# Mixture-of-experts phase of a fused long-convolution kernel: expert results kept in SBUF over the dispatched rows, in four chunks of groups

## The chip, the cores and the metric

One core of a Trainium2 chip runs the whole program. The metric is the device time in microseconds (us); the kernel before takes 2235.25 us, the median of three runs (2234.15 to 2236.55).

## What is computed

Two layers on x of 8192 tokens by 512, each with a residual and a layer norm. The first is a gated long convolution (a transform of length 16384, written as matrix products). The second, to which the change belongs, is a mixture of 32 x 4 = 128 small experts, in float32:

```
grouped = x.reshape(1, 256, 32, 512)                       # 256 groups of 32 tokens
logits  = einsum('bgtd,des->bgtes', grouped, controller) + tie
perm    = (logits == max(logits over t))                   # each expert takes one token of a group
dispatched   = einsum('bgtd,bgtes->bgesd', grouped, perm)  # its row, for each group and expert
inner        = relu(einsum('bgesd,desf->bgesf', dispatched, f1) + bias)   # 32 hidden values
intermediate = einsum('bgesf,esfd->bgesd', inner, f2)
out          = einsum('bgesd,bgtes->bgtd', intermediate, perm)
x = layernorm(x + out)
```

## The kernel before

The program runs four phases one behind the other, `front_phase`, `frequency_phase`, `output_phase` and `experts_phase`; each is one block in which the five engines have streams of their own, ordered by hand through semaphores. A phase begins when all streams of the last have ended.

At the end of `output_phase` the choices stand in `k_shared` (K, 128 experts by 8192 tokens): `choose(u)` on VectorE writes ones and zeros over the logits. `turn_take(v)` on TensorE transposes them to tokens by experts, `keep_took` copies these from PSUM, and `store_unit` on SyncE (SP) writes them to the scratch tensor TOOK in HBM.

`experts_phase` before works in `STEPS` = 4 steps: two halves of the groups (`GH` = 128) times two halves of the experts (`EH` = 64). A step is

- a **dispatch stage**: for each pair of token tiles `dispatch(c, j)` multiplies the tile by the choices, in two row strips of 64 (two groups in one product, so `pick` is padded with zeros by GpSimd at L1435). The result is x at the chosen tokens, turned: dimension on partitions. `keep_tile` (L1527) copies it from PSUM to `taken`.
- a **layer stage** over `QH` = 16 quads of experts: `layer1(c, i)` (L1472) 16 products in four column strips of 32, each with 128 groups as columns; `hidden` (L1580) adds the bias and cuts at zero; `layer2(c, i)` (L1484) four products of 512 columns in four row strips; `keep_out` (L1534) copies 2 x 1024 columns to `out`; SP stores 1 MB to the scratch tensor I (L1408) and loads the weights of a later quad (L1341).

From the third step on, the tiles of the first half are combined in between: `combine(m)` (L1498) multiplies rows of I, loaded back from HBM, by the choices (TAKE, stored to HBM and loaded back as well), and `add`, `moments`, `root`, `scale`, `finish` make the layer norm and ScalarE issues the store of the output. The second half is combined behind the last step. PSUM has three bank pairs `pd` for dispatch, shared with the layers, and two banks `pc` for combine.

Of the kernel before, what the change touches and what calls it, by code (L numbers as in the profile page):

```python
# [878 lines left out]
def output_phase(nc, sem, A, S, K, O):  # L879
# [5 lines left out]
    NZ, NR, NK = 3, 6, 4  # L885
    with ExitStack() as ctx:
# [3 lines left out]
        def ps(name, shape):  # L890
# [18 lines left out]
        took = [sb(f"took{s}", [P, 2, 8, ES // 2]) for s in range(NK)]  # L909
# [4 lines left out]
        pt = [ps(f"pt{s}", [P, 4, ES]) for s in range(2)] + pc  # L914
# [25 lines left out]
        def _(sp):  # L940
# [31 lines left out]
            def store_unit(u):  # L972
                for b in range(2):
                    sp.wait_ge(took_ok[b], ONE + u + 1)
                sp.dma_start(S["TOOK"][:, :, 8 * u:8 * u + 8, :].rearrange("h p m e -> p h (m e)"),
                             took[u % NK][:].rearrange("p h m e -> p h (m e)")).then_inc(took_st[u % NK], 16)

# [10 lines left out]
            for u in range(UNITS):  # L988
                store_unit(u)
            for s in range(NR):  # L990
                sp.wait_ge(x1_st[s], ONE + 16 * len(range(s, TILES, NR)))
            for s in range(NK):
                sp.wait_ge(took_st[s], ONE + 16 * UNITS // NK)
# [15 lines left out]
        def _(pe):  # L1009
# [35 lines left out]
            def turn_take(v):  # L1045
                pe.wait_ge(take_ok, ONE + UNITS + v // 2 + 1)
                if v == 2:
                    pe.wait_ge(c_used, ONE + TILES)
                if v >= 4:
                    pe.wait_ge(took_ok[v % 2], ONE + v // 2 - 1)  # L1050
                for b in range(4):
                    g = v * UG // 2 + 2 * b
                    m = pe.transpose(pt[v % 4][:, b, :], logit[:, g:g + 2].rearrange("p g r t -> p (g r t)"), ident[:])
                m.then_inc(t_ps, 1)

# [9 lines left out]
            for v in range(2 * UNITS):  # L1065
                turn_take(v)

        def keep_took(eng, copy, v):

            u, b = v // 2, v % 2  # L1070
            eng.wait_ge(t_ps, ONE + v + 1)
            if u >= NK:
                eng.wait_ge(took_st[u % NK], ONE + u // NK * 16)
            copy(took[u % NK][:, :, 4 * b:4 * b + 4].rearrange("p h m e -> p m h e"),
                 pt[v % 4][:].rearrange("p m (h e) -> p m h e", h=2)).then_inc(took_ok[b], 1)

        @block.scalar
        def _(act):
# [44 lines left out]
            for u in range(UNITS):  # L1123
                keep_took(act, nc.scalar.copy, 2 * u)

        @block.vector
        def _(dve):
# [50 lines left out]
            def choose(u):  # L1178
                half, g = u // UNITS, u % UNITS * UG
                by_group = logit[:, g:g + UG, half, :]  # L1180
                dve.wait_ge(top_ok, ONE + (half + 1) * HALF)
                dve.tensor_tensor(by_group, by_group,
                                  top[half][:, g:g + UG].rearrange("p (g a) -> p g a", a=1).to_broadcast([P, UG, GT]),
                                  ALU.is_equal).then_inc(take_ok, 1)

            for n in STEPS:
# [11 lines left out]
                for u in chosen(n):  # L1198
                    choose(u)
                    if u > UNITS:  # L1200
                        keep_took(dve, dve.tensor_copy, 2 * (u - UNITS - 1) + 1)
            keep_took(dve, dve.tensor_copy, 2 * UNITS - 1)

def experts_phase(nc, sem, A, S, K):

    GH = P
    NH = G // GH
    EH = ES // 2  # L1210
    TH = GH * GT // P
    QH = EH // 4
    NF = 4
    STEPS = NH * 2
    NO, NI, NR = 3, 2, 4
    PH = TH // 2
    ND = 3
    NX = 8
    WEIGHTS_OVER = (6, 7)
    TILES_OVER = (0, 1, 2, 3, 4, 5)  # L1220
    NP, NK = 2, 3
    NW = TH // 4
    IN_DISPATCH = (3, 6, 9, 12, 15)
    IN_LAYERS = tuple(i for i in range(QH) if i % 3 != 2)
    NT0 = NT // NH
    NL = 8
    LW = 5 * D + P
    with ExitStack() as ctx:
        def sb(name, shape, dt=F32):
            return ctx.enter_context(nc.sbuf_tensor("e_" + name, shape, dt))  # L1230

        taken = sb("taken", [P, DT * EH * GH])
        bias = sb("bias", [P, Q])
        eps = sb("eps", [P, 1])
        inter = [K[:, s * 4 * D:(s + 1) * 4 * D].rearrange("p (g d) -> p g d", g=4) for s in range(NI)]
        xt = [sb(f"xt{s}", [P, 2, D]) for s in range(2)]
        pick = [sb(f"pick{s}", [P, 2, 2 * EH]) for s in range(NP)]
        picked = [sb(f"picked{s}", [P, 4, EH]) for s in range(NK)]
        side = sb("side", [P, 2])
        ff = [sb(f"ff{s}", [P, 2, D])[:] for s in range(2)] + [  # L1240
            K[:, s * 2 * D:(s + 1) * 2 * D].rearrange("p (a d) -> p a d", a=2) for s in WEIGHTS_OVER]
        hid = [sb(f"hid{s}", [P, GH]) for s in range(2)]
        out = [sb(f"out{s}", [P, 4, D]) for s in range(NO)]
        take = [sb(f"take{s}", [P, P]) for s in range(NI)]
        res = [K[:, (NI * 4 + s) * D:(NI * 4 + s + 1) * D] for s in range(NR)]
# [44 lines left out]
        def res_of(m):  # L1290

            if m < NT0:
                return res[m % NR]
# [463 lines left out]
```

## Time and profile before

| | |
|---|---|
| runs | 2234.15, 2235.25, 2236.55 us |
| span of the profiled execution | 2229.5 us (no time of its own is listed for it; its span is 5.75 us under the median run) |
| `experts_phase`, from its first DMA at 1552.6 us | 676.9 us |
| TensorE / VectorE / ScalarE / GpSimd busy | 85% / 63% / 42% / 23% of the span |
| HBM traffic | 309.8 MB read, 201.6 MB written |
| mean granted TensorE clock | 0.916 of full |

Times in rows are counted in us from the start of the span. In a row of the timeline the columns are start, length, engine, line, operation, output<-inputs, sizes; in brackets stands the idle time ahead and who ended it. A float32 matmul is two records in the trace; a transpose is one. A row with x32 spans from the first record's start to the last one's end.

### The profile page before, as it was taken

What the parts mean: (1) busy time and instruction counts of PE and PEld (TensorE: products, weight loads), DVE (VectorE), ACT (ScalarE), POOL (GpSimd) and SP (SyncE); (2) the same over time, 40 slices, a digit from 0 to 9 for tenths busy, and PEclk for the clock granted to TensorE, in tenths of its full rate; (3) what the DMA queues carried; (4) which work ended last, traced back from release to release, by engine and by line L of the source; (5) the groups of instructions that cost most, each with busy time, mean ns of one, the idle gap of its engine ahead of it and who ended that gap; (6) DMA issues with size and microseconds to landing.
All of it is one profiled execution on the core that took longest, in us unless ns stands there. A gap on an engine that the chain in (4) does not pass through costs nothing. (4 is left out here: it accounts for less than half of the span.)

```text
span 2229.5 us, 34871 instructions
## 1 busy us (share of the span) xinstructions
PE 1895.0 (85%) x12342; PEld 1285.3 (58%) x12342; DVE 1405.8 (63%) x2748; ACT 933.4 (42%) x1755; POOL 513.0 (23%) x410
## 2 busy tenths in 40 slices
PE   7999999999999699999969999996757676576444
PEld 6777777777777443444458888885636352352000
DVE  5877777877778454555558889885434354354344
ACT  4444444444444344444445555552323232242222
POOL 0100010001000044454455555551302020020000
PEclk9999999999999899999999999998889797697555
DMA  5134233333333577888767777773997999999999
GB/s 167 67 116 140 100 114 114 126 116 114 107 114 113 175 202 226 221 243 229 208 196 248 246 245 237 237 243 136 356 392 286 383 336 413 405 326 413 373 391 344
DMA packets 287298, 513.73 MB, mean 230 GB/s; under 512 B 26480, under 2 KB 105366, under 8 KB 278806
## 3 DMA queue, kind: packets, MB, share of 16 engines
q1 hardware_dynamic: 277909, 494.71, 65.8%
q10 hardware_dynamic: 9216, 16.78, 2.0%
q8 instruction: 101, 1.65, 0.3%
q14 instruction: 72, 0.58, 0.1%
HBM read 309.78 MB, written 201.62 MB: 229 GB/s over the span
## 5 line engine op out<-in xcount | busy, mean ns | idle before, releaser
L90 PE MATMUL p_pu<-p_xT_high,p_win_high 128*128 128x512 f32 (+1 forms) x816 | 329.9, 404 | 14.2 <-DVE p_win_low L85 12.0
L91 PE MATMUL p_pu<-p_xT_high,p_win_low 128*128 128x512 f32 (+1 forms) x816 | 313.3, 384 | 0.0
L92 PE MATMUL p_pu<-p_xT_low,p_win_high 128*128 128x512 f32 (+1 forms) x816 | 313.1, 384 | 0.0
L447 ACT ACTIVATE p_t<-p_pu,p_tbias,p_taps 128x512 f32<-128x512 f32 (+1 forms) x192 | 146.5, 763 | 358.2 <-PE p_pu L92 357.3
L85 POOL TENSOR_TENSOR p_xT_low<-p_xT,p_xT_high 128x2048 fp32r<-128x2048 f32 (+1 forms) x16 | 71.3, 4456 | 618.0 <-ACT p_xT_high L80 618.0
L564 DVE SCALAR_TENSOR_TENSOR p_t<-p_pu,p_taps,p_t 128x256 f32<-128x256 f32 (+1 forms) x384 | 208.6, 543 | 6.8
L849 POOL TENSOR_TENSOR q_y<-q_y 128x512 f32<-128x512 f32 x128 | 160.2, 1270 | 194.8 <-DVE q_y L870 194.8
L90 PEld LDWEIGHTS p_pu<-p_xT_high,p_win_high 128*128 128x128 f32 x816 | 155.4, 190 | 46.8 <-DVE p_xT_low L85 10.2
L92 PEld LDWEIGHTS p_pu<-p_xT_low,p_win_high 128*128 128x128 f32 x816 | 154.9, 190 | 32.8
L91 PEld LDWEIGHTS p_pu<-p_xT_high,p_win_low 128*128 128x128 f32 x816 | 155.4, 190 | 25.4
L870 DVE TENSOR_TENSOR q_y<-q_pg,q_v 128x512 f32<-128x512 f32 x256 | 158.0, 674 | 2.1 <-PE q_pg L779 1.8
L1435 POOL TENSOR_SCALAR e_pick<-e_picked,e_side 128x128 f32<-128x128 f32 x128 | 75.4, 602 | 350.2 <-PE e_pd L1460 307.0
L1527 DVE COPY e_taken<-e_pd 128x1024 f32<-128x1024 f32 x64 | 78.4, 1225 | 116.7 <-PE e_pd L1460 116.5
L1534 ACT COPY e_out<-e_pd 128x1024 f32<-128x1024 f32 x64 | 64.7, 1011 | 192.8 <-PE e_pd L1484 192.8
L754 PE MATMUL q_pv<-q_av,f_fwd 128*64 128x512 f32 x512 | 127.0, 618 | 17.4 <-DMA q_ah<-s_SH 17.4
L85 DVE TENSOR_TENSOR q_h_b<-q_ph,q_h_a 64x256 fp32r<-64x256 f32 (+1 forms) x64 | 26.8, 419 | 180.6 <-ACT q_h_a L80 180.6
L1460 PE MATMUL e_pd<-e_pick,e_out 64*128 64x128 f32 x1536 | 100.1, 289 | 47.7 <-DMA e_out<-s_X 31.1
L371 PE MATMUL p_ps<-k_shared,p_dft 128*128 128x512 f32 x256 | 133.8, 604 | 3.4 <-ACT k_shared L463 2.7
L1002 POOL TENSOR_TENSOR o_gate<-t_x,t_grow_c 128x512 f32<-128x512 f32 x64 | 94.4, 1474 | 182.1 <-DVE o_y L1137 168.5
L1017 PE MATMUL o_pc<-t_idft,o_zin 128*128 128x128 f32 x1024 | 126.3, 277 | 11.5 <-DMA o_zin<-s_Z 11.5
L823 ACT COPY q_z<-q_pz 128x512 f32<-128x512 f32 x128 | 68.7, 589 | 158.9 <-PE q_pz L788 158.9
L564 DVE SCALAR_TENSOR_TENSOR p_t<-k_shared,p_taps,p_t 128x128 f32<-128x128 f32 x192 | 96.9, 508 | 60.7 <-ACT p_t L447 60.2
(144 smaller groups left out, 3773.7 us busy)
## 6 DMA issues: line engine op xcount, KB each, us to landing
s_I<-e_out SPq DMA_DIRECT2D x64, 1024.0 KB, 8.5
q_av<-s_SV SPq DMA_DIRECT2D x64, 512.0 KB, 4.3
s_Z<-q_z SPq DMA_DIRECT2D x128, 256.0 KB, 3.2
o_zin<-s_Z SPq DMA_DIRECT2D x64, 512.0 KB, 3.9
k_shared<-s_I SPq DMA_DIRECT2D x32, 1024.0 KB, 11.9
e_taken<-s_I SPq DMA_DIRECT2D x32, 1024.0 KB, 11.5
e_out<-s_X SPq DMA_DIRECT2D x48, 512.0 KB, 8.6
s_X<-p_t SPq DMA_DIRECT2D x64, 256.0 KB, 2.3
```

The costliest lines, as they stand in the source:

```text
L85: return eng.tensor_tensor(low, x, high.bitcast(F32), ALU.subtract)
L90: pe.matmul(out, a[0], b[0], start=start, stop=False)
L91: pe.matmul(out, a[1], b[0], start=False, stop=False)
L92: return pe.matmul(out, a[0], b[1], start=False, stop=stop)
L371: pe.matmul(pz[n % 2][:], dft[i % 2][:, j, r, :], vt[i % 2][:, j, :], start=True, stop=True).then_inc(s_ps, 1)
L447: nc.scalar.activation(t[r][m % 2][:, c], pu[(W + n) % 3][:, c], ACT.Identity, bias=tbias[:, w:w + 1], scale=taps[:, w, 2:3]).then_inc(t_o ...
L564: return dve.scalar_tensor_tensor(to, src.rearrange("p (a n) -> p a n", n=N1) if len(src.shape) == 2 else src, taps[:, w, tap:tap + 1], to ...
L754: m = pe.matmul(pv[r][a * B:(a + 1) * B, :], fwd[:, 1 if 2 * p + a else 0, r * B:(r + 1) * B], av[s][:, a, :], start=True, stop=True)
L849: pool.tensor_tensor(y[p % NY][:, r, :], y[p % NY][:, r, :], y2[p % NT2][:, r, :], (ALU.subtract, ALU.add)[r]).then_inc(y_ok, 1)
L870: dve.tensor_tensor(into, pg[k % NG][:], v[p % NV][:, half, :], ALU.mult).then_inc(g_used, 1)
L1017: m = pe.matmul(pc[n % 2][:, k, :], zin[s][:, r, k * P:(k + 1) * P], idft[s][:, r, :], start=(r == 0), stop=(r == 1))
L1460: m = pe.matmul(pd[:, b, h, k].rearrange("p e g -> p g e"), x[r, a, k * P:(k + 1) * P], chosen[r, a, :].rearrange("p (g e) -> p g e", g=2) ...
```

## The change

`output_phase` ends with `choose`: `turn_take`, `keep_took`, `store_unit` and TOOK are gone. The scratch tensors TAKE and I are gone too. `experts_phase` is written anew, with `CHUNKS` = 4 chunks of `GC` = 64 groups (`TC` = 16 tiles) and all 128 experts (32 quads) in each:

- `choices(c, b)` transposes four tiles of K, ScalarE copies them to `picked`; there is no padding and GpSimd has no work.
- `dispatch(c, m)` takes one tile in four row strips of 32, 16 products of 128 columns, into two bank pairs that are both complete only at its end. It is copied to `rows`, laid out dimension on partitions, then group, then expert.
- `layer1(c, i)` makes 16 products of 64 columns; its moving operand is `rows[:, k, :, 4i+e]`, one number every 512 bytes, and it writes every second column of `ph`. The other columns stay zero (`clear`), and `hidden` keeps them zero through `back`, so that `layer2(c, i)` makes 8 products of 128 columns in two row strips of 64, each of two experts. The copy of a quad (ScalarE for even i, VectorE for odd) writes over the dispatched rows it came from.
- `turn(c, n)` transposes the results of two groups (8 transposes); the copy `it` is what `combine` multiplies. Turns, dispatch of the next chunk and combine are interleaved tile by tile; behind the fourth chunk stand turns and combine alone.
- The order in which all these take the three PSUM bank pairs, and which engine copies each, stands in `numbered()`.

The core of the diff (new lines; the old functions are described above):

```
+            def dispatch(c, m):
...
+                to = [bank_pair(number["send", c, 2 * m + h]) for h in range(2)]
+                for k in range(DT):
+                    for g in range(4):
+                        r = slice(g * GT, (g + 1) * GT)
+                        w = pe.matmul(to[g // 2][:, g % 2, k * P:(k + 1) * P], x_tile(c, m)[r, k * P:(k + 1) * P],
+                                      picked[(4 * c + b) % 3][r, m % PT, :], start=True, stop=True)
...
             def layer1(c, i):
...
-                                      rows[:, k, 4 * i + e, :], start=(k == 0), stop=(k == DT - 1))
-                m.then_inc(h_ps[s], 1)
+                        x = pe.matmul(to[r, :, e % 2], ff[w][:, 0, k * P + e * EF:k * P + (e + 1) * EF],
+                                      rows[:, k, :, 4 * i + e], start=(k == 0), stop=(k == DT - 1))
+                x.then_inc(h_ps, 1)
...
             def layer2(c, i):
...
+                to = bank_pair(number["quad", c, i])
+                pe.wait_ge(hid_ok, ONE + n + 1)
+                for k in range(DT):
+                    for h in range(2):
+                        r = slice(h * 2 * EF, (h + 1) * 2 * EF)
+                        x = pe.matmul(to[:, h, k * P:(k + 1) * P], ff[w][r, 1, k * P:(k + 1) * P], hid[s][r, :],
+                                      start=True, stop=True)
...
+            def turn(c, n):
+                to = bank_pair(number["turn", c, n])
+                for g in range(2):
+                    for k in range(DT):
+                        x = pe.transpose(to[:, g, k * P:(k + 1) * P], rows[:, k, 2 * n + g, :], ident[:])
...
+                for m in range(TC + 1):
+                    if c and m < TC:
+                        turn(c - 1, 2 * m)
+                        turn(c - 1, 2 * m + 1)
+                    if c < CHUNKS and m:
+                        dispatch(c, m - 1)
+                        if m in (PT, 2 * PT):
+                            choices(c, m // PT + 1)
+                    if c and c < CHUNKS and m < TC:
+                        combine(c - 1, m)
+                    if c == CHUNKS and m:
+                        combine(c - 1, m - 1)
...
+            def load_weights(n):
+                if n >= NF:
+                    b = n - NF
+                    sp.wait_ge(u_ps, ONE + number["quad", b // Q, b % Q] + 1)
+                sp.dma_start(ff[n % NF][:], A["ffn_f"][:, n % Q]).then_inc(ff_in[n % NF], 16)
```

How the order changes on TensorE (the names are output<-inputs, x counts products of one line behind each other). First the layers; before, in the first step:

```order
L1472 MATMUL e_pd<-e_taken,e_ff 32x128 x32
L1484 MATMUL e_pd<-e_ff,e_hid 128x512 x4
L1472 MATMUL e_pd<-e_taken,k_shared 32x128 x16
L1484 MATMUL e_pd<-e_ff,e_hid 128x512 x4
L1472 MATMUL e_pd<-e_taken,k_shared 32x128 x16
```

and in the changed kernel, in the first chunk:

```order
L1374 MATMUL e_pq<-e_taken,e_ff 32x64 x32
L1386 MATMUL e_pun<-e_hid,e_ff 128x128 x8
L1374 MATMUL e_pq<-e_taken,e_ff 32x64 x16
L1386 MATMUL e_pun<-e_hid,e_ff 128x128 x8
L1374 MATMUL e_pq<-e_taken,e_ff 32x64 x16
```

The alternation is the same; a quad of layer 1 now has half as many columns in each product, one of layer 2 twice as many products of a quarter of the columns, and there are 128 quads in place of 64.

Second, TensorE where combining overlaps with dispatch; before, in the third step:

```order
L1460 MATMUL e_pd<-e_pick,e_out 128x2x64 x48
L1498 MATMUL e_pc<-k_shared,e_take 32x512 x4
L1460 MATMUL e_pd<-e_pick,e_out 128x2x64 x16
L1460 MATMUL e_pd<-e_pick,e_xt 128x2x64 x32
L1498 MATMUL e_pc<-k_shared,e_take 32x512 x4
```

and in the changed kernel, in the dispatch stage of the second chunk:

```order
L1394 MATMUL e_pun<-e_ident,e_taken 128x128 x16
L1359 MATMUL e_pun<-e_picked,e_xt 128x128 x16
L1407 MATMUL e_pq<-e_it,k_shared 32x512 x4
L1394 MATMUL e_pun<-e_ident,e_taken 128x128 x16
L1359 MATMUL e_pun<-e_picked,e_xt 128x128 x16
L1407 MATMUL e_pq<-e_it,k_shared 32x512 x4
```

Each tile now brings 16 transposes (L1394) ahead of its dispatch (L1359) and a combine behind it (L1407). Third, ScalarE at the same place in the changed kernel, two tiles:

```order
L1460 COPY e_it<-e_pun 128x1024
L1469 ACTIVATE e_std<-e_mv,e_eps 128x1
L1460 COPY e_taken<-e_pun 128x2x4x128
L1473 ACTIVATE e_res<-e_res,e_mv 128x512
L1476 DMA out<-e_res 128x512
L1460 COPY e_taken<-e_pun 128x2x4x128
L1460 COPY e_it<-e_pun 128x1024
L1469 ACTIVATE e_std<-e_mv,e_eps 128x1
L1460 COPY e_taken<-e_pun 128x2x4x128
L1473 ACTIVATE e_res<-e_res,e_mv 128x512
L1476 DMA out<-e_res 128x512
L1460 COPY e_it<-e_pun 128x1024
```

The copy of a turn (`e_it`) stands behind the output's scaling and its store, and in every second tile behind a second copy of dispatched rows.

## Rows read from the trace of the kernel before

**Rows 1.** The page: chain that ended last, by line.
```profile
DMA k_shared<-in_L_ffn_f 5%; PE e_pd L1460 4%; DMA e_ff<-in_L_ffn_f 4%; SPq L1362 3%; PE e_pd L1484 2%; PE e_pd L1472 1%; DVE e_out L1534 1%; DMA e_take<-s_TAKE 1%; SPq L1365 1%; DMA e_out<-s_X 1%; SPq L1361 1%; DMA s_I<-e_out 1%; DMA e_taken<-s_TAKE 1%; ACT e_taken L1527 0%; PE e_pc L1498 0%
```

**Rows 2.** Busy time by stage: window, its length, busy us of each engine, PEclk, DMA, GB/s.
```profile
1559.10:1603.20 44.10, 36.40 (x588) 34.92 (x592) 21.52 (x19) 17.20 (x17) 19.90 (x34) 0.90 0.98 359
...
1826.10:1943.30 117.20, 69.08 (x792) 31.09 (x792) 47.42 (x94) 31.17 (x42) 2.36 (x4) 0.74 1.02 398
1943.30:1983.00 39.70, 34.12 (x488) 28.33 (x489) 23.88 (x35) 17.75 (x22) 14.13 (x24) 0.96 0.90 326
...
2089.00:2229.50 140.50, 61.93 (x256) 6.46 (x256) 56.60 (x162) 36.27 (x65) 0.00 (x0) 0.50 1.01 372
```

**Rows 3.** DMA issues: KB each, median us to landing.
```profile
s_I<-e_out SPq DMA_DIRECT2D x64, 1024.0 KB, 8.5
q_av<-s_SV SPq DMA_DIRECT2D x64, 512.0 KB, 4.3
...
k_shared<-s_I SPq DMA_DIRECT2D x32, 1024.0 KB, 11.9
...
e_ff<-in_L_ffn_f SPq DMA_DIRECT2D x32, 512.0 KB, 8.5
```

**Rows 4.** Timeline, end of `output_phase` and start of `experts_phase`.
```profile
1532.32 1.29 DVE L1182 TENSOR_TENSOR k_shared<-k_shared,o_top 128x512 f32<-128x512 f32 x2
...
1541.43 1.09 PE L1053 MATMUL o_pt<-t_ident,k_shared 128*128 128x128 f32 x8 [0.18 <-DVE k_shared L1182]
...
1543.77 0.69 DVE L1074 COPY o_took<-o_pc 128x512 f32<-128x512 f32 x1 [0.51 <-PE o_pc L1053]
1552.63 0.33 SPq L1335 DMA_DIRECT2D e_picked<-s_TOOK  x1
...
1553.99 0.43 SPq L1373 DMA_DIRECT2D e_bias<-in_L_ffn_bias  x1
```

**Rows 5.** Issue to landing, 512 KB each: first `p_dft`, then the experts' weights (L1341).
```profile
DMA to landing us min/median/max: 3.6/6.9/8.1
...
DMA to landing us min/median/max: 5.8/9.2/15.7
```

**Rows 6.** Timeline of a layer stage where no DMA is waited for.
```profile
1706.61 1.08 PE L1472 MATMUL e_pd<-e_taken,k_shared 128*32 128x128 f32 x32
...
1708.12 1.14 PE L1484 MATMUL e_pd<-e_ff,e_hid 32*128 32x512 f32 x8 [0.43 <-DVE e_out L1534]
...
1709.32 1.01 ACT L1534 COPY e_out<-e_pd 128x1024 f32<-128x1024 f32 x1 [1.56 <-PE e_pd L1484]
1709.32 1.23 DVE L1534 COPY e_out<-e_pd 128x1024 f32<-128x1024 f32 x1 [1.09 <-PE e_pd L1484]
1710.46 0.34 DVE L1580 TENSOR_SCALAR e_hid<-e_pd,e_bias 128x128 f32<-128x128 f32 x1
...
1710.69 1.14 PE L1484 MATMUL e_pd<-k_shared,e_hid 32*128 32x512 f32 x8 [0.42 <-DVE e_out L1534]
```

**Rows 7.** Timeline of a dispatch stage with a combine in it.
```profile
1965.41 0.68 DVE L1589 TENSOR_TENSOR k_shared<-e_pc,k_shared 128x512 f32<-128x512 f32 x1
...
1966.44 0.81 ACT L1547 ACTIVATE k_shared<-k_shared,e_mv 128x512 f32<-128x512 f32 x1 [2.06 <-DVE e_mv L1596]
...
1967.25 1.23 DVE L1527 COPY e_taken<-e_pd 128x1024 f32<-128x1024 f32 x1
...
1967.67 0.29 ACT L1543 ACTIVATE e_std<-e_mv,e_eps 128x1 f32<-128x1 f32 x1 [0.42 <-ACT k_shared L1547]
1967.87 1.90 ACT L1527 COPY e_taken<-e_pd 128x1024 f32<-128x1024 f32 x2
...
1971.95 2.06 PE L1460 MATMUL e_pd<-e_pick,e_out 64*128 64x128 f32 x32 [1.87 <-issue]
...
1973.94 1.07 PE L1498 MATMUL e_pc<-k_shared,e_take 128*32 128x512 f32 x8
```

**Rows 8.** Busy time in two stretches in which TensorE had transposes alone.
```profile
1534.00:1538.00 4.00, 4.00 (x23) 3.79 (x22) 2.97 (x5) 1.52 (x3) 0.00 (x0) 0.60 0.40 151
1538.00:1542.00 4.00, 3.33 (x27) 2.62 (x26) 4.00 (x8) 1.75 (x3) 0.00 (x0) 1.00 1.00 368
```

More of the change, by code:

```diff
@@ L1230, in sb @@
             return ctx.enter_context(nc.sbuf_tensor("e_" + name, shape, dt))
[L1232 to L1245, printed above, removed]
+        taken = sb("taken", [P, DT * GC * ES])
+        rows = taken[:].rearrange("p (k n e) -> p k n e", k=DT, e=ES)
+        ident, side, eps = sb("ident", [P, P]), sb("side", [P, 2]), sb("eps", [P, 1])
+        bias, nbias, back = sb("bias", [P, Q]), sb("nbias", [P, Q]), sb("back", [P, Q, 2])
+        ff = [sb(f"ff{s}", [P, 2, D]) for s in range(NF)]
+        xt = [sb(f"xt{s}", [P, D]) for s in range(NX)]
+        it = [sb(f"it{s}", [P, 2, D]) for s in range(NI)]
+        picked = [sb(f"picked{b}", [P, PT, ES]) for b in range(3)]
+        hid = [sb(f"hid{s}", [P, GC * 2]) for s in range(2)]
+        res = [sb(f"res{s}", [P, D]) for s in range(NR)]
         stats = [sb(f"stats{s}", [P, 6]) for s in range(2)]
@@ new lines, in bank_pair, with all_taken, choices @@
+            def bank_pair(u):
+                if u >= NU:
+                    pe.wait_ge(taken_ok[taker[u - NU]], ONE + taken_by[u - NU])
+                return pun[u % NU]
+            def all_taken(u):
+                for on in (ON_ACT, ON_DVE):
+                    pe.wait_ge(taken_ok[on], ONE + taker[:u + 1].count(on))
+            def choices(c, b):
+                to = bank_pair(number["pick", c, b])[:, 0]
+                for m in range(PT):
+                    t = (c * TC + b * PT + m) * P
+                    x = pe.transpose(to[:, m * ES:(m + 1) * ES], K[:, t:t + P], ident[:])
+                x.then_inc(u_ps, 1)
@@ L1517, in _ @@
[L1517 to L1534 removed]
+            pe.wait_ge(consts, ONE + 48)
@@ new lines, in take @@
+            def take(kind, c, n):
+                keep(dve, dve.tensor_copy, ON_DVE, kind, c, n)
+            clear(0)
+            dve.wait_ge(consts, ONE + 48)
+            step = Steps(dve, prep)
+            step(dve.tensor_scalar(nbias[:], bias[:], 0.0, None, ALU.min))
+            step(dve.tensor_scalar(bias[:], bias[:], 0.0, None, ALU.max))
+            for x in range(2):
+                step(dve.scalar_tensor_tensor(back[:, :, x], bias[:], side[:, x:x + 1], nbias[:], ALU.mult, ALU.add))
@@ new lines, in _ @@
+            step(dve.tensor_tensor(bias[:], bias[:], nbias[:], ALU.add))
+            dve.tensor_scalar(nbias[:], bias[:], -1.0, None, ALU.mult).then_inc(back_ok, 1)
+            dve.wait_ge(back_ok, ONE + 1)
+            for c in range(CHUNKS + 1):
+                behind = 1 if c < CHUNKS else 2
+                for m in range(TC + behind):
+                    j = (c - 1) * TC + m - behind
+                    if c and m < TC:
+                        take("turn", c - 1, 2 * m + 1)
+                    if c and m >= behind:
+                        scale(j)
+                    if c < CHUNKS and m:
+                        take("send", c, 2 * m - 1)
+                    if c and behind - 1 <= m < TC + behind - 1:
+                        add(j + 1)
+                        if c < CHUNKS and m == TC - 1:
+                            clear(c)
+                        moments(j + 1)
+                if c == CHUNKS:
+                    break
@@ L1618, in _ @@
                 hidden(c, 0)
-                for i in range(QH):
-                    if i + 1 < QH:
+                for i in range(Q):
+                    if i + 1 < Q:
                         hidden(c, i + 1)
-                    keep_out(dve, dve.tensor_copy, 1, c * QH + i)
-                    m = in_layers(c, i)
-                    if m is not None:
-                        normed(m)
-            for m in range(NT0, NT):
-                normed(m)
-            scale(NT - 1)
+                    take("quad", c, i)
```

548 lines of the change are left out of this document (219 added, 329 removed).

## The prediction

> **What bounds the kernel now.** I read the chain of waits first. Its largest pieces are DMAs: the experts' weights, the issue of the loads behind the last step, the choices loaded back [rows 1]. The windows by stage say the same. In a layer stage the DMA engines are full (share 1.02, 398 GB/s) while TensorE is busy 69 of 117 us; behind the last step it is 62 of 140.5 us, with a granted clock of 0.50 throughout [rows 2]. The issue list shows with what: 1 MB of results stored and loaded back for each quad or tile [rows 3]. Only the first dispatch stage has both full, TensorE 36.4 and DMA 0.98 of 44.1 us [rows 2]. In a layer stage without a DMA wait a quad takes 2.57 us, layer 2 to layer 2, and that is not TensorE either: copy and product share PSUM banks and alternate [rows 6]. So the traffic through HBM goes, and what counts is whether TensorE and the two copying engines do the new, larger work in under 677 us.
>
> **Prices.** Copies: ScalarE 1.01 us (0.95 behind one another, [rows 7]), VectorE 1.23 [rows 6]. A product's end to its copy is 0.06 us (1709.26 to 1709.32), a copy's end to the product that waits for its bank 0.14 (1710.55 to 1710.69) [rows 6]. Four column strips of 32 take 32 records in 1.08 us, eight rounds of four, some 0.11 each; four row strips run side by side as well, 8 records of 512 columns in 1.14 [rows 6]; two row strips take 2.06 for 32 records, 16 rounds [rows 7]. Eight transposes take 1.09 alone [rows 4] and 0.86 in a run (0.11 each, less the 0.2 in which the last drains). A combine is 1.07, output scaling to the next work of ScalarE 1.23 (1966.44 to 1967.67), VectorE's share of a layer norm 1.84 (1965.41 to 1967.25) [rows 7].
>
> **Start.** Transposes, copies and the TOOK store vanish: VectorE chooses eight times without a break, 1532.3 + 8 x 0.69 = 1537.9. Before, 8.0 us passed from the last copy (1544.5) to the first DMA of the phase (1552.6) [rows 4]; I give 4 of them to the store's landing and 4 to the change of phases, which remains: first DMA at 1541.9. The bias, fourth in line before and fifth now, landed 5.1 us behind it in the chain, so 5.6; eight transposes and two copies, TensorE cold: dispatch from **1549.8**, 9.3 us earlier than now.
>
> **Dispatch, first chunk.** 32 records in four row strips, eight rounds: 1.15 us with the first load of weights. The next tile needs a bank pair that ScalarE copies now: 1.15 + 0.06 + 1.01 + 0.14 = 2.4 us a tile, x16 = 38 us. At half clock it is 3.4 and 54. TensorE is busy half of this stage, and 62 of 140.5 us busy went with clock 0.50 [rows 2]; I take 50. Removed against it is the first dispatch of now, 44 us for half the experts.
>
> **Layer stages**, 4 x 32 quads. Layer 1: eight rounds of four with 64 columns, each between 0.055 (half the columns, half the time) and 0.11 (no gain); I take 0.11, the row that exists, 0.9 to 1.08 us. Layer 2: eight rounds of two, 1.03. With the drain of one part under the start of the next and 0.1 for each change of strips, 2.05 us a quad. Hidden under it: ScalarE 1.01 and VectorE 1.23 + 2 x 0.35 for two quads (4.1 us), three bank pairs deep. The weights: 512 KB for every quad, four buffers; from the end of a quad's layer 2 to the layer 1 that reuses the buffer lie two periods, 4.1 us. A load of that size takes 3.6 us at best [rows 5] and 4.3 in the median of the second phase [rows 3]; 3.9 is just covered, and this is the cover that goes first. A stage is 32 x 2.05 + 2.4 (first product, last copy) = 68 us; four: **272 us**. Today's third layer stage takes 117.2, with 64 of 128 experts for half the groups and eleven combines [rows 2].
>
> The Trainium skill, "TensorE: Matmul & The Clock Gate" (Part 1), states a floor of about 25 ns from matmul to matmul however few the columns. By it layer 1 takes 0.8 us a quad and the sum hardly moves; no row here has 64 columns in strips.
>
> **Dispatch with turns and combine**, 48 tiles. TensorE: 2 x 0.86 + 1.05 + 1.0 = 3.8 us. ScalarE in two tiles: five copies, two roots of 0.2, two outputs: 8. VectorE: three copies and twice 1.84: 7.4. None fills the period; a wait does. `dispatch` holds until its second bank pair, that of this tile's first turn, is copied, and ScalarE comes to that copy behind the last tile's: dispatch 1.15 + 0.06, copy 1.01, output 1.23, turn copy 1.01, 0.14 = 4.6 us; in every second tile one more copy, 5.6. Mean 5.1 x 16 = 82 us, plus 4 for fill, end and some cold stretches: **86 us**, three times 258. TensorE has 3.8 of 5.1 us of work; in the stage now nearest to it, busy 34.1 of 39.7, the clock was 0.96 [rows 2], so some of it may go cold.
>
> **Last chunk.** Turns and combine alone: three copies, two roots, two outputs of ScalarE in two tiles, 5.9 us, with waits 3.2 a tile, 51 + 5 fill + 3 cold = **59 us**, against 140.5 us now [rows 2].
>
> The Trainium skill, "TensorE: Matmul & The Clock Gate" (Part 4), states that transposes do not count as TensorE work for the clock. By it this stage would run at half clock. The trace disagrees: with transposes alone the clock went from 0.60 to 1.00 [rows 8].
>
> **Sum.** 1549.8 + 50 + 272 + 258 + 59 + 2.5 for the last store = 2191.3 us of span, against 2229.5. The median stands 5.75 above that span: **2197 us**, 1.7% less.
>
> **Rivals.**
> - *Layer 1 reads slowly* (slower). Its moving operand is one number in 512 bytes; every product of now reads contiguous columns. If a round took two of now (0.22 us), layer 1 were 1.95 and a quad 2.9: +0.85 x 128 = +109, **2306 us**. It decides from 2.35 us a quad, that is (2235 - 2197)/128 = 0.3 more, a round of 0.15 us. For it: nothing here reads so. Against: the strided writes of L1527 cost VectorE the same 1.23 as the contiguous ones of L1534 [rows 6, 7]. The Trainium skill, "Advanced Engine Details and Errata" (Memory Cachelines), states that SBUF wants two accesses in a 16-byte line for full speed, and layer 1 would have one.
> - *Weights become the wait* (slower). If a load takes 5.8 us, the least beside today's traffic [rows 5], a quad takes (5.85 + 4.1)/4 = 2.5: +57, **2254 us**. Against: the load is 512 KB in 2 us, 256 GB/s, where 398 were moved.
> - *The four row strips of dispatch run in pairs*, as the two of now do: 2.07 in place of 1.15, x 64 tiles: +59, **2256 us**. Against: layer 2 of now runs four strips of 32 rows together [rows 6].
> - *Half clock in the middle stages*: work of 7.6 in place of 5.1 us a tile, +120, **2317 us**, or a part of it.
> - *All covers hold* (faster): layer 1 with half rounds and weights in 3.6 us give 1.9 a quad, stages of 62 (-24), a warm first stage (-12), 83 and 56 (-12): **2149 us**.
>
> **Chances.** Forecast 0.55 (own range 2170 to 2225), all covers hold 0.13, slow reads 0.08, weights 0.08, pairs 0.08, half clock 0.05, no change by cancelling 0.03. Faster by over 0.2% (the least this measurement can tell) 0.68, within 0.2% 0.04, slower 0.28. The range 2140 to 2265 leaves out slow reads, half clock and a little below.
>
> **What would show it.** Layer stages of 68 us and DMA share near 0.65 in them; a wait of L1374 for `e_ff` would mean the weights, a longer row of L1374 without a wait the reads. L1359 x32 in 1.1 us or 2.1. Tiles in the middle stages 4.6 and 5.6 us apart with dispatch waiting for ScalarE's copy; a last stage of 59 us at a clock near 1. TensorE waiting less than a tenth of a layer stage. I am wrong if a stage of layers is over 80 us or a middle stage over 100.

## The result, and the profile after

| | before | after |
|---|---|---|
| runs | 2234.15 to 2236.55 us | 2321.2 to 2322.65 us |
| median | 2235.4 us (4 runs) | **2322.55 us** (4 runs) |
| span of the profiled execution | 2229.5 us | 2320.8 us |

The ratio is 1.0384, 95% interval 1.0369 to 1.0398: slower, where 2197 us was forecast. (One run of e4 below took 2653.09 us at a granted clock of 0.75, far from its other three; it is left out of the time and the ratio of e4.) Below the busy lines of the page of the changed kernel, and what it says of HBM:

```profile
PE 2160.8 (93%) x16950; PEld 1592.6 (69%) x16950; DVE 1478.5 (64%) x2850; ACT 1021.3 (44%) x1859; POOL 436.6 (19%) x282
...
HBM read 251.13 MB, written 126.12 MB: 163 GB/s over the span
```

The traffic went as it should: 377 MB against 511 before. The chain of waits is no longer led by DMAs [rows 1] but by layer 1 (chain by engine and by line, then the group of L1374):

```profile
PE 23%; ACT 6%; issue 2%; DMA 1%; DVE 1%; ACTq 1%; SPq 0%; DVEq 0%
PE e_pq L1374 11%; PE e_pun L1386 6%; PE e_pun L1359 4%; ACT e_taken L1460 3%; ACT e_it L1460 2%; PE e_pun L1394 1%; ACT e_res L1473 1%; DMA e_ff<-in_L_ffn_f 1%; PE e_pq L1407 1%; ACTq L1476 1%; DVE e_taken L1460 0%; PE e_pun L1347 0%; DVE e_it L1460 0%; DMA e_bias<-in_L_ffn_bias 0%; ACT e_ff L1473 0%
...
L1374 PE MATMUL e_pq<-e_taken,e_ff 128*32 128x64 f32 x4096 | 274.8, 450 | 11.5 <-DVE e_taken L1460 8.1
```

Windows of the changed kernel, in the columns of [rows 2]: first dispatch, two layer stages, most of a middle stage, the last stage.

```profile
1548.50:1599.00 50.50, 33.56 (x528) 28.80 (x528) 20.25 (x22) 18.22 (x20) 0.00 (x0) 0.60 0.32 113
1599.70:1701.00 101.30, 100.35 (x1522) 84.53 (x1524) 30.72 (x47) 15.18 (x15) 0.00 (x0) 0.98 0.58 170
1705.00:1785.00 80.00, 64.74 (x892) 45.61 (x889) 57.86 (x103) 52.92 (x72) 0.00 (x0) 1.00 0.45 140
1786.80:1888.00 101.20, 100.71 (x1526) 84.98 (x1528) 30.91 (x47) 15.24 (x16) 0.00 (x0) 0.98 0.59 173
2262.00:2320.00 58.00, 48.39 (x384) 30.20 (x384) 39.67 (x89) 39.02 (x56) 0.00 (x0) 0.97 0.38 124
```

In a layer stage TensorE is busy without a break at nearly full clock, while DMA has 0.58. It waits for nobody; its own work is too long. That is the sign that the prediction had named for slow reads: a longer row of L1374 without a wait. The timeline shows which part (TensorE alone, two quads):

```profile
1651.25 1.16 PE L1386 MATMUL e_pun<-e_hid,e_ff 64*128 64x128 f32 x16
...
1652.34 2.17 PE L1374 MATMUL e_pq<-e_taken,e_ff 128*32 128x64 f32 x32
...
1654.44 1.16 PE L1386 MATMUL e_pun<-e_hid,e_ff 64*128 64x128 f32 x16
```

Layer 2 (L1386) takes 1.16 us. Layer 1 (L1374) takes 2.17 us for 32 records (2.14 to 2.18 in the other quads) of **64** columns; the same number of records with **128** columns took 1.08 before [rows 6]. With 0.12 of overlap the quad is 3.2 us.

### The profile page after: what moved, and what is told of

The parts are those of the page before. It is cut to its first block and busy times, and to the rows that moved or that the text cites. A ratio compares the mean times of both kernels' runs of the same rounds, so it can differ in the third digit from the quotient of the medians.

```text
span 2320.8 us, 44001 instructions
## 1 busy us (share of the span) xinstructions
PE 2160.8 (93%) x16950; PEld 1592.6 (69%) x16950; DVE 1478.5 (64%) x2850; ACT 1021.3 (44%) x1859; POOL 436.6 (19%) x282
## 5 line engine op out<-in xcount | busy, mean ns | idle before, releaser
L1460 ACT COPY e_taken<-e_pun 128x1024 f32<-128x1024 f32 x152 | 153.8, 1012 | 436.5 <-PE e_pun L1386 344.1
L1374 PE MATMUL e_pq<-e_taken,e_ff 128*32 128x64 f32 x4096 | 274.8, 450 | 11.5 <-DVE e_taken L1460 8.1
L1374 PEld LDWEIGHTS e_pq<-e_taken,e_ff 128*32 128x32 f32 x4096 | 218.0, 155 | 27.9 <-ACT e_taken L1460 10.2
L1520 DVE SCALAR_TENSOR_TENSOR e_hid<-e_pq,e_nbias,e_back 128x128 f32<-128x128 f32 x128 | 50.0, 391 | 234.4 <-PE e_pq L1374 234.4
L1460 DVE COPY e_taken<-e_pun 128x1024 f32<-128x1024 f32 x104 | 127.3, 1224 | 96.6 <-PE e_pun L1386 50.4
L1386 PEld LDWEIGHTS e_pun<-e_hid,e_ff 64*128 64x128 f32 x2048 | 124.0, 187 | 47.4 <-issue 47.4
L1394 PEld LDWEIGHTS e_pun<-e_ident,e_taken 128*128 128x128 f32 x1024 | 110.5, 140 | 55.1 <-issue 45.1
L1386 PE MATMUL e_pun<-e_hid,e_ff 64*128 64x128 f32 x2048 | 147.7, 284 | 0.0
```

The lines of the kernel that those rows point to most:

```text
L1374: x = pe.matmul(to[r, :, e % 2], ff[w][:, 0, k * P + e * EF:k * P + (e + 1) * EF], rows[:, k, :, 4 * i + e], start=(k == 0), stop=(k == DT ...
L1386: x = pe.matmul(to[:, h, k * P:(k + 1) * P], ff[w][r, 1, k * P:(k + 1) * P], hid[s][r, :], start=True, stop=True)
L1394: x = pe.transpose(to[:, g, k * P:(k + 1) * P], rows[:, k, 2 * n + g, :], ident[:])
L1460: copy(out, at).then_inc(taken_ok[on], 1)
```

## The stages, forecast against measured

From the first product of a stage to that of the next, in us (layer stages include their last copy, middle stages the first quad's wait for its rows):

| | forecast | measured | difference |
|---|---|---|---|
| start of dispatch, behind the first choices | 1549.8 | 1550.5 | +0.7 |
| first dispatch | 50 | 49.2 | -0.8 |
| four layer stages | 272 | 102.2 + 101.9 + 101.4 + 103.4 = 408.9 | **+136.9** |
| three middle stages | 258 | 84.9 + 84.8 + 84.7 = 254.4 | -3.6 |
| last stage and store | 61.5 | 57.8 | -3.7 |
| span | 2191.3 | 2320.8 | +129.5 |

The median stands 1.75 above the span where I had 5.75: 129.5 - 4 is the error of 125.5 us. One term holds all of it. The experiments therefore ask why 64 columns cost twice what 128 did, and what is left when they don't.

## Experiments

*Pitch* means here the distance from one number that a product reads of its moving operand to the next; in the changed kernel it is 512 bytes, or 128 numbers. The theories on record for the first four runs are S (this pitch), P (layer 1 writes every second column of PSUM), R (short products cost their issue or their weight load) and I (the reads meet the copies into the same tile). "Stages" are the four layer stages, first to last product, 102.0, 101.7, 101.2 and 101.7 us in the changed kernel. e1 to e3, e5 to e7, e9, e11 and e12 are one run each, and the ten runs of e13 spread over 12.5 us; the readings below therefore rest on the stages and on the rows of single quads, which agree within 0.05 us at full clock.

### Where the slowness sits: e1, e2, e3

`e1_k_pitch1` and `e2_k_pitch128` read another tile in the place of the rows, once contiguous, once at the old pitch (from the diff, both in one):

```
-                                      rows[:, k, :, 4 * i + e], start=(k == 0), stop=(k == DT - 1))
+                                      probe(k, i, e), start=(k == 0), stop=(k == DT - 1))
...
+            def probe(k, i, e):
+                b = (4 * k + e) % (L // (GC * s)) * GC * s       # s = 1 in e1, 128 in e2
+                return K[:, b:b + GC * s].rearrange("p (n s) -> p n s", s=s)[:, :, (4 * i + e) % s]
```

> The changed kernel, but the moving operand of layer 1 is 64 contiguous numbers of the choices (k_shared) instead of one number in 512 bytes of the rows; everything else stays, the experts' results are not computed. S, the read pitch is what makes layer 1 slow: a quad of layer 1 takes 0.5 to 1.1 us in place of 2.1, a layer stage about 68 us in place of 102, time 2160 to 2190 us. P, the writes to every second PSUM column are: no change, 2322 us. R, a product of 64 columns costs as much as its issue and weight load, whatever it reads: no change, 2322 us. I, reads of the tile that the copies write to collide with these: about 2186 us, since k_shared is not written in the phase.

> Control of the one before: layer 1 reads k_shared too, one number in 512 bytes as the changed kernel does from its rows; the experts' results are not computed. S, P and R: as the changed kernel, layer stages of 102 us, 2322 us. I: about 2186 us, as with contiguous reads.

Measured: e1 2213.70 us, stages 73.4, 72.5, 72.8, 74.0; e2 2328.75 us, stages 102.0, 102.0, 101.7, 101.9. Of e2, a quad's layer 1 (TensorE):

```profile
1638.49 2.16 PE L1378 MATMUL e_pq<-k_shared,e_ff 128*32 128x64 f32 x32
```

e1 stays above the 2160 to 2190 us that were expected of it under S: layer 1 fell as S says, the stages did not reach 68 us. `e3_psum_flat` keeps the rows and writes PSUM contiguously:

```
-                        x = pe.matmul(to[r, :, e % 2], ff[w][:, 0, ...
+                        x = pe.matmul(ph[s][r, 0:GC], ff[w][:, 0, ...
```

> The changed kernel, but layer 1 writes 64 contiguous PSUM columns instead of every second of 128, so the hidden values stand in the wrong places; reads stay at 512 bytes. P: a quad of layer 1 falls to about 1 us, time about 2186 us. S, R and I: no change, 2322 us.

Measured: 2324.07 us, stages 102.4, 101.6, 102.4, 101.6. So P is out as the cause. R is out as well: in e1 the same 32 products of 64 columns, with the same weight loads, take 0.65 us (timeline of e1, TensorE):

```profile
1632.09 0.65 PE L1378 MATMUL e_pq<-k_shared,e_ff 128*32 128x64 f32 x32 [1.00 <-DMA e_ff<-in_L_ffn_f]
1632.68 1.16 PE L1390 MATMUL e_pun<-e_hid,e_ff 64*128 64x128 f32 x16
```

And I is out, because e2 reads a tile into which nothing is written in this stage, and is as slow. The pitch of the read is shown as the cause. The first row of e1 shows what comes next: a wait for the weights. In the second layer stage of e1 (groups of TensorE):

```profile
L1390 PE MATMUL e_pun<-e_hid,e_ff 64*128 64x128 f32 x512 | 39.1, 294 | 0.0
L1378 PE MATMUL e_pq<-k_shared,e_ff 128*32 128x64 f32 x1024 | 21.9, 229 | 17.7 <-DMA e_ff<-in_L_ffn_f 15.0 <-DVE e_taken L1464 2.7
```

15.0 of 72.5 us are waits for weights, though DMA has a share of 0.74. Even with cheap reads my 68 us would have been missed, by 5.

### How the time grows with the pitch: e5, e6, e9, e12

The probe of e1 with other pitches `s`. In e9 each chunk has one, in e12 each half chunk.

> The dose of the read pitch, the lower step. As e1 (layer 1 reads 64 numbers of the choices, so its results are not the experts'), but every second number: 8 bytes from number to number, two numbers in 16 bytes. Theory L (what counts is how many of the numbers lie in the same 16-byte line, and two are enough): layer 1 as at 4 bytes, 0.65 us a quad, layer stages 73 us, 2214 us. Theory G (the cost grows with the distance): between 0.65 and 2.14 us, at 8 of 512 bytes close to 0.65, so it can't be told from L here, but by e6. Theory H (any pitch but contiguous is slow): 2.14 us, stages of 102, 2323 us.

> The dose, the upper step: every fourth number of the choices, 16 bytes from number to number, one in each 16-byte line. Theory L: the full slowness, layer 1 in 2.14 us, layer stages of 102 us, 2323 us, the same as at 512 bytes. Theory G (grows with the distance): 16 of 512 bytes is little, layer 1 at most 0.8 us, stages near 73, 2215 us.

> The dose between 16 and 512 bytes, one pitch for each chunk: layer 1 reads 64 numbers of the choices (results not the experts') 32, 64, 128 and 256 bytes apart in chunk 1, 2, 3 and 4. Measured so far for the 32 records of a quad: 0.65 us at 4 bytes, 0.67 at 8, 1.12 at 16, 2.14 at 512. Theory L alone (one number in a line of 16 bytes costs double, and that is all) can't give 2.14, so there is a second step or a slope. Theory D (doubling: the time doubles with each doubling of the pitch until it reaches 2.14): 2.14 us already at 32 bytes, stages of 102 us in all four chunks, 2323 us. Theory B (a second step at a power of two that the 512 bytes share, banks for instance): 1.12 us up to some pitch and 2.14 beyond it, stages of 77 and 102. Theory F (the far distance costs gradually): values between, 1.3, 1.5, 1.8, 2.0.

> Is it the distance or the power of two? Measured so far for a quad's 32 records: 1.15 us at a pitch of 64 bytes or 16 numbers, 1.57 at 32 numbers, 2.15 at 64 and 2.14 at 128 numbers. Here layer 1 reads 64 numbers of the choices (results not the experts') at a pitch of 65 and 66 numbers in the first and second half of chunk 1, 68 and 72 in chunk 2, 129 and 130 in chunk 3, 48 and 96 in chunk 4. Theory B (places at a power of two apart collide, as banks would): odd and near-odd pitches cost 1.12 to 1.15, as at 16 to 64 bytes; 72 and 96 (8 and 32 times an odd number) something between, and padding each group's row in SBUF would be a repair. Theory F (the distance itself): 2.14 us at 65, 66, 68, 72, 96, 129 and 130 alike and about 1.8 at 48, all stages 100 us or more, 2320 us; padding would bring nothing. Under B the stages are 75 to 80 us and the whole near 2230.

Measured: 2213.36, 2229.07, 2258.41 and 2235.18 us. A quad's layer 1, by pitch in numbers of 4 bytes (a typical row of each at full clock; rows of one pitch differ by some 0.05):

| pitch | 1 | 2 | 4 | 8 | 16 | 32 | 64 | 128 | 65, 66 | 68, 72 | 129, 130 | 48 | 96 |
|---|---|---|---|---|---|---|---|---|---|---|---|---|---|
| us | 0.65 | 0.67 | 1.12 | 1.13 | 1.15 | 1.57 | 2.15 | 2.14 | 1.15, 1.17 | 1.13, 1.14 | 1.15, 1.18 | 1.15 | 1.59 |

Four of these rows, from the timelines of e6 (pitch 4), e9 (pitches 32 and 64) and e12 (pitch 65):

```profile
1632.62 1.11 PE L1378 MATMUL e_pq<-k_shared,e_ff 128*32 128x64 f32 x32
```

```profile
1937.23 1.58 PE L1379 MATMUL e_pq<-k_shared,e_ff 128*32 128x64 f32 x32
...
2113.37 2.16 PE L1379 MATMUL e_pq<-k_shared,e_ff 128*32 128x64 f32 x32
```

```profile
1608.71 1.15 PE L1379 MATMUL e_pq<-k_shared,e_ff 128*32 128x64 f32 x32
```

There are two steps. The first lies between 8 and 16 bytes: two numbers in 16 bytes are enough, one is not, and from there to 64 bytes nothing changes. That is the rule of theory L; but L had put the whole slowness, 2.14 us, at 16 bytes, and G at most 0.8 us, so neither size expected of e6 came. H, G and D are out. The second step is no matter of distance (F is out): 256 bytes cost 2.15, 260 cost 1.15; 96 numbers (32 times an odd number) cost what 32 do, 48 what 16 do. The power of two in the pitch decides, as theory B has it, though B had foreseen neither the 1.58 us in between at 128 bytes nor that 72 numbers cost no more than 65. That it is banks in the memory was only argued; what is shown is the pattern. Layer 1 runs in four column strips side by side in every run here, so whether the numbers of one strip collide with each other or with those of its neighbours is not shown either.

### Undoing it in the kernel itself: e13

```
-        taken = sb("taken", [P, DT * GC * ES])
-        rows = taken[:].rearrange("p (k n e) -> p k n e", k=DT, e=ES)
+        taken = sb("taken", [P, DT * GC * (ES + 1)])
+        rows = taken[:].rearrange("p (k n e) -> p k n e", k=DT, e=ES + 1)[:, :, :, 0:ES]
```

> The changed kernel with one number of padding behind each group's 128 experts in the tile of dispatched rows, 516 in place of 512 bytes from group to group; nothing else is changed and it computes what the reference does. Theory B (layer 1 is slow because places a power of two apart collide): layer 1 takes 1.15 us a quad in place of 2.14, the weights' round trip becomes a part of the wait, layer stages 75 to 78 us as in e12 and e9, 2323 - 4 x 25.5 = 2221 us (2215 to 2232), about 0.6% faster than before. The copies into the rows may lose something, since pieces of 8 and 16 bytes no longer start at multiples of 16: if the two quad and send copies take 1.5 in place of 1.01 us, dispatch and middle stages of 90 instead of 82 us and 2250 us. Rival (the reads of e5 to e12 were of the choices, ones and zeros, and the rows behave otherwise): stages stay at 102, 2323 us.

Measured: 2227.96 us (2221.88 to 2234.39, 10 runs), ratio to before 0.997, interval 0.9954 to 0.9986; stages 78.2, 78.0, 76.8, 78.2. One unused number per group takes back 95 us and turns the change from slower to slightly faster. Timeline, and the groups of the second layer stage:

```profile
1632.51 1.18 PE L1374 MATMUL e_pq<-e_taken,e_ff 128*32 128x64 f32 x32
```

```profile
L1374 PE MATMUL e_pq<-e_taken,e_ff 128*32 128x64 f32 x1024 | 37.0, 299 | 8.9 <-DMA e_ff<-in_L_ffn_f 6.1 <-DVE e_taken L1460 2.7
```

In dispatch and the middle stages ScalarE's copies kept their price (1018 ns in the middle stage; 1012 before the padding), and the middle stages their 81.9 us. In the layer stages its copy of a quad's results, which writes pieces of 16 bytes, now 516 bytes apart, went from 1012 to 1178 ns; VectorE's stayed at 1225. Of ScalarE in the second layer stage of e13:

```profile
L1460 ACT COPY e_taken<-e_pun 128x1024 f32<-128x1024 f32 x16 | 18.8, 1178 | 59.8 <-PE e_pun L1386 59.8
```

So there is a loss for pieces off a multiple of 16 bytes, a third of the one that I had priced, and it costs no time: ScalarE stands idle for 59.8 us of this stage. The rival (rows behave otherwise than choices) is out.

### The other layout: e4

Here the rows are laid out dimension, expert, group, so that layer 1 reads contiguously and whoever writes the rows, or turns them, strides:

```
-        rows = taken[:].rearrange("p (k n e) -> p k n e", k=DT, e=ES)
+        rows = taken[:].rearrange("p (f n a) -> p f n a", n=GC, a=1)     # f = k * ES + e, FK = ES
...
-                        x = pe.transpose(to[:, g, k * P:(k + 1) * P], rows[:, k, 2 * n + g, :], ident[:])
+                        x = pe.transpose(to[:, g, k * P:(k + 1) * P], rows[:, k * FK:(k + 1) * FK, 2 * n + g, 0], ident[:])
```

> The rows are laid out dimension, expert, group, so that layer 1 reads 64 contiguous numbers; the price is that each transpose of the turns loads its stationary operand at one number in 256 bytes, and that the copies write single numbers 256 bytes apart. Everything is computed. S: layer stages of 68 us in place of 102, 2186 us, if strided stationary loads cost nothing; if they cost a transpose 0.1 us more, the 1024 of them bring back up to 100 us, 2290 us. P and R: 2322 us or more. I: 2322 us.

Measured: 2329.64 us (2328.66 to 2330.47, three runs), ratio 1.042, interval 1.04 to 1.0441: above the 2290 us that S gave at most, and by the time alone what P and R had foreseen. The stages tell it apart. They are 71.5, 73.1, 72.6, 77.0: 112 us won. The dispatch stages, first to last product, went from 49.3, 81.9, 81.8, 81.8, 50.0 to 73.9, 110.2, 108.9, 106.8, 57.4: 112 us lost. The waits between the stages grew by 6 us more. Groups of the first middle stage, changed kernel and e4:

```profile
L1394 PEld LDWEIGHTS e_pun<-e_ident,e_taken 128*128 128x128 f32 x225 | 24.4, 140 | 11.7 <-issue 10.1 <-ACT e_taken L1460 1.7
L1460 ACT COPY e_taken<-e_pun 128x1024 f32<-128x1024 f32 x20 | 20.2, 1012 | 17.9 <-PE e_pun L1359 14.9 <-PE e_pun L1394 2.9
```

```profile
L1461 ACT COPY e_taken<-e_pun 128x1024 f32<-128x1024 f32 x15 | 31.8, 2123 | 16.4 <-PE e_pun L1361 14.3 <-ACT e_res L1474 2.1
...
L1396 PEld LDWEIGHTS e_pun<-e_ident,e_taken 128*128 128x128 f32 x167 | 25.6, 256 | 10.7 <-issue 7.1 <-ACT e_taken L1461 3.6
```

ScalarE's copy doubled (1012 to 2123 ns) and a weight load at 256 bytes from number to number went from 140 to 256 ns. VectorE's copy of dispatched rows went from 1.22 to 2.4 us and more. Here the cost of the pitch moved with the stride, to the engines that stride by single numbers.

### The wait behind it: e7, e8, e10, e11, e14

`e7` splits the weights of e1, so that each half waits only for the products that used it:

```
+                if n >= NF:
+                    sp.wait_ge(h_ps, ONE + n - NF + 1)
+                sp.dma_start(ff[n % NF][:, 0], A["ffn_f"][:, n % Q, 0]).then_inc(ff_in[n % NF], 16)
...
-                sp.dma_start(ff[n % NF][:], A["ffn_f"][:, n % Q]).then_inc(ff_in[n % NF], 16)
+                sp.dma_start(ff[n % NF][:, 1], A["ffn_f"][:, n % Q, 1]).then_inc(ff2_in[n % NF], 16)
```

> e1 (contiguous reads of the choices in layer 1, results not the experts') with each quad's weights loaded in two DMAs of 256 KB: the half for layer 1 waits for layer 1 of four quads earlier, the half for layer 2 for its layer 2, and TensorE waits for each by itself. Theory W (in e1 the round trip of the weights sets the quad, 2.27 us: buffer free, 3.6 us or more to land, two periods later the layer 1 that needs it): with three or four periods of room the wait goes and TensorE's work is left, 0.65 + 1.16 + some 0.15 for changes: 1.95 to 2.0 us a quad, layer stages 63 to 65 us in place of 73, 2174 to 2184 us in all. Rival B (the weights are slow because of the rate of HBM or of the queue, not the round trip): twice the DMAs at the same bytes, stages of 73 or more, 2214 us or above.

Measured: 2173.55 us, stages 63.3, 65.0, 66.0, 63.6. Of the 40 us to e1, 35 lie in the layer stages and the rest in a first dispatch that had more of the full clock. Twice the DMAs and the same bytes in less time: the round trip, not a rate, was the wait of e1. A half lands hardly sooner than the whole did (in the median 4.3 against 4.5 us); it is asked for earlier.

`e8` has ScalarE gather the rows of a quad for layer 1, up to three quads ahead (`near` are the turn tiles):

```
+                nc.scalar.copy(near[n % NI].rearrange("p f k n a -> p (k n) f a"),
+                               rows[:, :, :, 4 * i:4 * i + 4].rearrange("p k n (f a) -> p (k n) f a", a=2)).then_inc(near_ok, 1)
```

`e10` is e8 with the loads of x and residuals one at a time instead of five at quad 16, `e11` is e8 with whole weights, `e14` is e13 (padding, no gather) with halves and the spread loads.

> A repair that computes what the reference does. While the layers run, ScalarE copies each quad's dispatched rows, up to three quads ahead, into the turn tiles (free in this stage), laid out so that layer 1 reads at 8 bytes from number to number; the weights come in halves as in e7. If theory L holds and the copy costs ScalarE about the 1.0 us of its others, ScalarE has 3.0 us of work for two quads of 3.9 to 4.0, TensorE stays the bound: layer stages 65 us (the first gather stands open with 2 us), dispatch as in the changed kernel, 2180 to 2190 us: faster than before by 2%, where the changed kernel is 3.8% slower. If the gather reads slowly (1.9 us, as strided single writes did in e4; it reads 16 bytes of each 512), ScalarE has 4.8 us for two quads, 2.4 us a quad, stages of 79, 2235 us: no change against before. If reads at 8 bytes are slow (H): stages of 102, 2325 us.

> e8 (ScalarE gathers each quad's rows for layer 1, weights in halves, computes what the reference does), and the five loads of x tiles and residuals that SP issues in one go behind quad 16 are issued one in every fourth quad, from quad 8 on. In e8 TensorE stands 3.5 us idle at that place for the weights queued behind them (and loses some clock after it). Theory: the hole goes in every layer stage, 3.5 to 5 us each: stages of 60 to 62 us, 2187 - 4 x 4 = 2171 us (2166 to 2176), ratio to before 0.971. Rival: each spread load makes a small hole of its own (each lies under a weights load in the queue), same sum, 2187 us.

> e8 without the weights in halves: the gather alone on the changed kernel (it computes what the reference does). Theory: as e1, where reads were contiguous and the weights' round trip set the quad: stages 72 to 75 us instead of 102, with some 2 to 4 us more in front of each for the first gather: 2323 - 4 x 25 = 2223 us (2215 to 2230). Rival: the gather holds the quads by itself, then no difference to e8's 2187.

> e13 with the weights in halves (as e7) and the loads of x and residuals spread (as e10), no gather by ScalarE. TensorE's work is left as the bound of the quad: 1.15 + 1.16 less the overlap of 0.12 is 2.19 us, x 32 and 1 to 2 us for the first: stages 71 to 72.5 us, 2323 - 4 x 30 = 2203 us (2196 to 2212), ratio 0.985. The gather of e10 should stay ahead of it (stages of 63 us, 3 to 4 us of gap in front of each: 2177), by 0.5 us a quad against that gap.

| | median, us | ratio to before, 95% | stages, us |
|---|---|---|---|
| e8 | 2187.26 | 0.9777 (0.9753 to 0.9802) | 66.2, 66.6, 63.9, 63.5 |
| e10 | **2176.86** | **0.9732 (0.9712 to 0.9753)** | 62.7, 63.6, 63.4, 61.2 |
| e11 | 2217.8 (one run) | | 76.7, 74.8, 72.9, 70.7 |
| e14 | 2197.29 | 0.9834 (0.9808 to 0.986) | 69.2, 70.1, 69.8, 69.6 |

Nothing is left out of the computation in these four. The times expected of e8, e11, e13 and e14 held, and e7 came out 0.5 us below its range; the stages of e14, 69.2 to 70.1 us, are shorter than the 71 to 72.5 expected. In e8 one long hole is left in each layer stage, behind the five loads (timeline of e8):

```profile
1801.62 1.08 PE L1382 MATMUL e_pq<-e_it,e_ff 128*32 128x64 f32 x32 [3.54 <-DMA e_ff<-in_L_ffn_f]
```

e10 takes off 10.4 us of the 16 expected and ends 0.9 above its range: the stages stay 4 to 7 us over their TensorE work (57.1 busy of 63.6 us in the second, clock 0.97), in waits for weights that are shorter and more, so its rival holds in part. A quad of e10 and one of e14, layer 1 to layer 1:

```profile
1632.47 0.68 PE L1381 MATMUL e_pq<-e_it,e_ff 128*32 128x64 f32 x32
...
1634.17 0.68 PE L1381 MATMUL e_pq<-e_it,e_ff 128*32 128x64 f32 x32
```

```profile
1632.01 1.17 PE L1377 MATMUL e_pq<-e_taken,e_ff 128*32 128x64 f32 x32
...
1634.20 1.16 PE L1377 MATMUL e_pq<-e_taken,e_ff 128*32 128x64 f32 x32
```

1.70 and 2.19 us, TensorE's own work in both. In the stage of e14 TensorE waits for no weights at all (its second layer stage):

```profile
L1377 PE MATMUL e_pq<-e_taken,e_ff 128*32 128x64 f32 x1024 | 36.8, 298 | 2.7 <-DVE e_taken L1464 2.7
```

e10 is the best version that computes everything: 2.7% faster than before and 6.3% faster than the changed kernel.

## Why the prediction was wrong, point by point

- **The failed step** is in "Layer stages": "each between 0.055 [...] and 0.11 (no gain); I take 0.11, the row that exists". A round measured 2.14 / 8 = 0.27 us; read contiguously (e1) it would have been 0.65 / 8 = 0.08, inside the bounds. The row that exists reads contiguous columns; "no gain" is no upper bound for an operand that is laid out otherwise. The bounds were made for the number of columns and not for the pitch, the one thing about which the text itself said that nothing here reads so. With it a quad is 2.14 + 1.16 - 0.12 = 3.18 us, and 32 of them are the 102 us measured.
- **The rival *layer 1 reads slowly*** is what happened, with a price too small: 0.22 a round and 2306 us against 0.27 and 2322.6. It decided from 0.15, and was far past it. Its 0.08 rested on one argument, that strided writes cost VectorE the same 1.23 [rows 6, 7]. That copy writes pieces of two neighbouring numbers. e4, which writes single ones, shows the price that the argument missed.
- The Trainium skill, "Advanced Engine Details and Errata" (Memory Cachelines), asks for two accesses in a 16-byte line for full speed. The runs agree with it at the pitches on both sides: 0.67 us at 8 bytes, 1.12 at 16. It accounts for 0.5 of the 1.5 us lost per quad; nothing in that section gives the second step, which is the other 1.0.
- The Trainium skill, "TensorE: Matmul & The Clock Gate" (Part 1), states a floor of some 25 ns between matmuls. By it layer 1 could not be under 0.8 us. In e1 it took 0.65 for 32 records, 20 ns each; the trace disagrees, for products in four column strips.
- **Weights.** "3.9 is just covered" was wrong in the direction that I had noted: with fast reads (e1) a load landed after 4.5 us in the median, and the quad stood at 2.27 us, not 2.05. In the changed kernel slow reads hid it (median landing 3.6 us, and two periods of 3.2 us to cover it).
- **Dispatch** held: L1359 takes x32 in 1.17 us, so the four strips run together and *pairs* is out. First dispatch took 49.2 for 50, its clock 0.60. That it is so close is luck in part: 50 was picked between 38 (full clock) and 54 (half), and the same dispatch code took 4 us more in e1 and e8, where the clock was 0.50 throughout.
- **Middle stages** held, by their mechanism too, with tiles 5.0 and 5.4 us apart where 4.6 and 5.6 were forecast. Dispatch waits for ScalarE's copy of the turn; the next tile starts at 1735.81 (timeline of the changed kernel):

```profile
1725.43 1.17 PE L1359 MATMUL e_pun<-e_picked,e_xt 32*128 32x128 f32 x32 [1.34 <-ACT e_it L1460]
...
1730.40 1.17 PE L1359 MATMUL e_pun<-e_picked,e_xt 32*128 32x128 f32 x32 [0.32 <-ACT e_it L1460]
```

- **Clock.** *Half clock in the middle* is out (1.00). The last stage, 32.9 us of transposes and 17.1 us of combine, had 0.97. By the statement of the Trainium skill, "TensorE: Matmul & The Clock Gate" (Part 4), that transposes don't count for the clock, it would have run at half clock; the trace doesn't show that, though with combines in between it tests the statement less sharply than [rows 8].
- *All covers hold* needs cheap reads and weights in time. e10 has both for the most part and takes 2177 us, 28 more than that rival's 2149 and 20 fewer than the forecast.

## What to carry to other kernels

When a layout is turned so that one engine may write in place, price the pitch of every operand that touches it, reads of the moving operand first, and let the range reach beyond the nearest row if no row has that pitch. For a float32 moving operand of TensorE, two numbers in each 16 bytes cost next to nothing (0.67 against 0.65 us), single ones 0.5 us per 32 short products here, and a pitch of a large power of two another 1.0, which one number of padding removes. Behind a bound that is removed look for the next: 35 us of the layer stages lay in weights that waited for both users of a buffer where each half has one (e1 against e7).

## What the runs showed of the hardware that I had not expected

- The second step of the read pitch: with 64 numbers read, 256 and 512 bytes cost 2.15 us, 260, 264, 516 and 520 cost 1.15 to 1.18, 128 and 384 bytes 1.57 and 1.59.
- Pieces are another matter than single numbers. ScalarE's gather in e10 reads pieces of 16 bytes at 512 and writes pieces of 8 in 1137 ns for 1024 numbers (mean of 128), against 1012 for its copies out of PSUM; its writes of single numbers 256 bytes apart took 1.9 to 2.5 us (e4, first middle stage), the copies of 16-byte pieces at 516 bytes 1178 ns (e13).
- Writing every second column of PSUM showed no cost. Without it the kernel took the same (2324.07 against 2322.55 us, e3), where the reads would have hidden a small one; but products of 64 columns that still write so took 0.65 us for 32 in e1, and the 128-column products in two row strips took 1.16 us for 16 both ways, writing so in the kernel before (L1460, at 1968.92) and contiguously in the changed one (L1386).
- A short hole costs more than itself. In e8 TensorE stood idle for 3.5 us at 1798 and then ran over 6 us at half clock, 1.2 in place of 2.4 GHz; behind the long holes of the other layer stages (3.0, 3.3 and 4.7 us) the clock was 0.50, 0.66 and 0.55 over the next 3.4 to 5.7 us. Shorter holes did not always do so: in the changed kernel the clock was 0.58, 1.00 and 0.60 in the 4 us behind the waits of 2.69 us ahead of its last three layer stages. The windows of the hole at 1798 and of what follows:

```profile
1798.30:1801.60 3.30, 0.00 (x0) 0.00 (x0) 1.04 (x1) 1.16 (x2) 0.00 (x0) 0.92 0.97 328
1801.60:1805.60 4.00, 3.98 (x80) 3.47 (x80) 0.35 (x1) 0.85 (x1) 0.00 (x0) 0.50 0.65 246
1805.60:1807.90 2.30, 2.30 (x34) 2.03 (x32) 0.48 (x2) 2.19 (x3) 0.00 (x0) 0.50 0.71 228
```
